# Setup of a fused attention and feed-forward kernel: the order of the small moves, of the value products and of GpSimd's work before the first block

## The reference, cut to what matters

```
x = x + L0_xattn(layernorm(x), ctx, mask)
q = hidden @ Wq.T + bq ; k = ctx @ Wk.T + bk ; v = ctx @ Wv.T + bv      # 16 heads of 16
attn = softmax(q k^T / sqrt(16) + mask) ; out = (attn @ v) @ Wo.T + bo
x = x + L0_ffn(layernorm(x))        # experts
x = x + L1_xattn(layernorm(x), ctx) # second attention
x = x + L1_ffn(layernorm(x))
```

## Time and profile before

| | us |
|---|---|
| median of three runs | 789.11 |
| lowest, highest | 788.72, 789.34 |
| the profiled execution, whole | 788.65 |
| its span in the trace | 786.4 |

### The profile page before, as it was taken

How to read it: one execution, slowest core, us unless ns; L and a number is a source line. 1 busy time by engine, 2 the same in 40 slices (tenths; PEclk the granted TensorE clock), 3 DMA queues, 4 the chain that set the end, 5 groups by cost and what they waited for, 6 DMA issues and landing times.

```text
span 786.4 us, 13553 instructions
## 1 busy us (share of the span) xinstructions
PE 730.7 (93%) x4372; PEld 548.4 (70%) x4372; DVE 645.4 (82%) x1546; ACT 513.6 (65%) x943; POOL 374.3 (48%) x323
## 2 busy tenths in 40 slices
PE   4799999999999999999998999999989999999995
PEld 3456666766558888888875555555558888888985
DVE  7658778777878878888887888998788999999995
ACT  3546556565654456555436777677778989989885
POOL 6374444334222223232214232222259999999884
PEclk9999999999999999999999999999999999999999
DMA  7975635564210000001047755755200000000001
GB/s 231 135 208 121 143 71 96 119 120 87 69 36 1 1 1 7 1 1 55 1 60 121 92 78 77 131 76 78 32 1 1 2 28 28 28 28 2 28 28 54
DMA packets 25101, 48.64 MB, mean 62 GB/s; under 512 B 3686, under 2 KB 7016, under 8 KB 24520
## 3 DMA queue, kind: packets, MB, share of 16 engines
q1 hardware_dynamic: 23366, 46.54, 30.6%
q10 hardware_dynamic: 1666, 1.24, 0.5%
HBM read 12.12 MB, written 4.19 MB: 21 GB/s over the span
## 4 chain that ended last, share of the span: by engine, by line
PE 53%; DVE 20%; issue 9%; ACT 7%; DMA 6%; POOL 4%; DVEq 0%; ACTq 0%; POOLq 0%
PE bank L141 15%; PE bank L649 7%; PE bank L413 6%; PE bank L436 6%; DMA qst<-mt 5%; PE bank L424 5%; PE bank L388 4%; DVE mx L342 4%; PE bank L416 3%; PE bank L812 3%; DVE fpart L768 3%; DVE x L617 2%; PE bank L391 2%; DVE fyl L780 2%; POOL fy L728 2%
## 5 line engine op out<-in xcount | busy, mean ns | idle before, releaser
L316 ACT ACTIVATE pt<-bank 77x512 f32<-77x512 f32 x256 | 141.0, 589 | 79.1 <-PE bank L416 59.3
L342 DVE TENSOR_REDUCE mx<-bank 128x4 f32<-128x308 f32 x256 | 108.6, 470 | 22.9 <-PE bank L391 12.3
L413 PE MATMUL bank<-qst,l_kst 128*77 128x512 f32 (+1 forms) x256 | 102.6, 416 | 16.8 <-DMA qst<-mt 10.5
L721 POOL TENSOR_TENSOR frise<-fg,fg 128x512 f32<-128x512 f32 x64 | 101.8, 1591 | 6.0 <-DVE fpart L768 0.8
L388 PE MATMUL bank<-l_kblk,qh 128*128 128x308 f32 x256 | 81.2, 339 | 7.6 <-DVE mx L342 6.4
L284 POOL TENSOR_TENSOR ol<-ot,oh 128x512 fp32r<-128x512 f32 x32 | 41.4, 1293 | 94.5 <-ACT oh L321 50.4
L103 POOL TENSOR_TENSOR rstd<-var,minus_half 128x4 f32<-128x4 f32 x32 | 34.8, 1088 | 102.5 <-DVE var L98 54.4
L617 DVE SCALAR_TENSOR_TENSOR x<-bank,eweight,x 128x256 f32<-128x256 f32 x192 | 79.5, 475 | 4.5 <-PE bank L649 4.2
L413 PEld LDWEIGHTS bank<-qst,l_kst 128*77 128x77 f32 (+1 forms) x256 | 36.5, 146 | 66.0 <-ACT pt L316 24.1
L114 ACT ACTIVATE xn<-x,shift,rstd 128x256 f32<-128x256 f32 (+1 forms) x128 | 67.0, 592 | 17.9 <-POOL shift L105 17.9
L812 PE MATMUL bank<-fw2h,fyh 128*128 128x256 f32 x256 | 73.3, 286 | 5.0 <-DVE fyl L780 4.7
(11 more groups left out here) (176 smaller groups left out, 2115.6 us busy)
## 6 DMA issues: line engine op xcount, KB each, us to landing
qst<-qh SPq DMA_DIRECT2D x64, 256.0 KB, 6.5
qst<-ql SPq DMA_DIRECT2D x32, 256.0 KB, 8.7
out<-x SPq DMA_DIRECT2D x8, 512.0 KB, 2.6
qst<-ml SPq DMA_DIRECT2D x8, 480.0 KB
x<-in_x SPq DMA_DIRECT2D x3, 1024.0 KB, 12.7
weights<-in_mlp_w SPq DMA_DIRECT2D x2, 1024.0 KB, 5.2
mraw<-in_mask SPq DMA_DIRECT2D x8, 154.0 KB
x<-in_x SPq DMA_DIRECT2D x2, 512.0 KB, 5.4
```

What stands on the lines that cost most here:

```text
L316: self.nc.scalar.activation(self.pt[0:T, i // 4 % 2, i % 4, :], self.bank_of(G, i)[0:T, :], ACT.Exp).then_inc(self.probs, 1)
L342: self.nc.vector.reduce_max(out, banks[u % len(banks)][:, 0:4 * T].rearrange("q (p par t) -> q p par t", p=2, par=2), AX.X).then_inc(self. ...
L413: last = self.nc.tensor.matmul(out, layer.kst[rows, layer.stack(c * HC + 2 * k + par), b * T:(b + 1) * T], self.qst[rows, self.slot(G), c ...
L721: self.nc.gpsimd.tensor_tensor(self.rise[:, k % 2, :], self.g1[:, k % self.R, :], self.g0[:, k % self.R, :], ALU.subtract).then_inc(self.r ...
```

## The change

Four engines' orders change; no instruction is added or dropped.

- SyncE: `load_mask` of block 1 and the move of block 0's maxima now come behind the first half (six `kst` copies and queries half 0); behind them the second half of the `kst` copies and queries half 1. The `x` loads stay behind those.
- GpSimd: the sixteen `kblk` instructions now wait for `kblk_ready` (the end of VectorE's own sixteen) in place of `kt_ready`, and come ahead of `invert(1)`; then `mask_parts(1)`, then `wol`. In the loop `mask_parts` is left out for G = 0.
- ScalarE: the first bank of values is copied ahead of `norm(1)`. In block 0 the two `leading` copies follow exponentials 1 and 2 in place of 0 and 1.
- TensorE: the value product of batch 0 comes ahead of block 0's queries, the other three stay. In block 0 the queries of block 1 follow scores 1 and 2 in place of 0 and 1.

```diff
@@ sync
                 for c in range(C):
+                    if c == 1:
+                        att.load_mask(sp, 1, d["mask"])
+                        att.stack_maxima(sp, 0)
                     for par in range(2):
                         ... # three kst copies
-                    if c == 0:
-                        att.stack_queries(sp, 0, 0)
-                att.stack_maxima(sp, 0)
-                att.stack_queries(sp, 0, 1)
-                att.load_mask(sp, 1, d["mask"])
+                    att.stack_queries(sp, 0, c)
@@ gpsimd
-                norm.invert(pool, 1)
-                pool.wait_ge(kt_ready, 1)
+                pool.wait_ge(kblk_ready, 1)
                 for head in range(H):
                     ... # kblk of batches 1 to 3
+                norm.invert(pool, 1)
+                att.mask_parts(pool, 1)
...
-                    if G + 1 < BLOCKS:
+                    if 0 < G < BLOCKS - 1:
                         att.mask_parts(pool, G + 1)
@@ scalar
-                norm.norm(act, 1)
-                act.wait_ge(v_clear, 2)
                 for k in range(2):
+                    if k == 1:
+                        norm.norm(act, 1)
+                    act.wait_ge(v_clear, 2)
                     act.wait_ge(v_done, k + 1)
...
-                        if h < C and n < BLOCKS:
+                        if G == 0 and h in (1, 2):
+                            att.leading(act, 1, h - 1)
+                        if G > 0 and h < C and n < BLOCKS:
                             att.leading(act, n, h)
@@ tensor
+                pe.wait_ge(vo_in, 64)
+                pe.wait_ge(cleared, 1)
+                values(0)
                 pe.wait_ge(wql_ready, 1)
...
                 att.turn_maxima(pe, 0, FIRST_MAX[0])
-                pe.wait_ge(vo_in, 64)
-                pe.wait_ge(cleared, 1)
-                for b in range(B):
-                    ... # one value product: four matmuls and a row of ones
+                for b in range(1, B):
+                    values(b)
...
-                        if i < C and n < BLOCKS:
+                        if G == 0 and i in (1, 2):
+                            att.queries(pe, l0, 1, i - 1)
+                        if G > 0 and i < C and n < BLOCKS:
                             att.queries(pe, l0, n, i)
```

More of the change, by code:

```diff
@@ L1504, in _, with values @@
                     norm.turn(pe, 0, c, att.W[c])
+                def values(b):
+                    bank = att.SC[b // 2][0:T, D * (b % 2):D * (b % 2) + D]
+                    for k in range(C):
+                        nc.tensor.matmul(bank, ctx[:, k, b * T:(b + 1) * T], wv0[:, k, :], start=(k == 0), stop=False)
+                    last = nc.tensor.matmul(bank, ones_row[:, :], rows[:], start=False, stop=True)
+                    if b % 2:
+                        last.then_inc(v_done, 1)
+                pe.wait_ge(vo_in, 64)
+                pe.wait_ge(cleared, 1)
+                values(0)
                 pe.wait_ge(wql_ready, 1)
```

## The result

The changed kernel takes 793.95 us in the median (792.96 to 795.41, 4 runs), the kernel before 788.91 beside it (787.91 to 789.34, 4 runs): ratio 1.0059 [1.0045, 1.0074], 5.0 us slower. The prediction was 787.4, in 783.0 to 790.2; the time lies above the range. It moved the way rival (c) said, and 2.7 us beyond that rival's 791.3.

The account below looks back on a forecast made before the run. It took score 0 of block 0, waiting for the maxima's move, and scarce DMA engines as the bound. Queue -2.6 and clock +0.9 gave -1.7 us: 788.65 to 786.95, median 0.46 above, so 787.4, range 783.0 to 790.2.

Parts of the forecast that it names:

- rival (c): Block 1's query copies become a burst at 127 instead of 191 GB/s: +2.2 us in sum, 791.3 us; chance 0.13.
- score 0 waited for the maxima's move behind the 47 rows: Block 0's head: with the maxima moved ahead, score 0 can start at 36.1 instead of 40.77, 4.7 us sooner.
- where each part of the setup would stand: Setup: `kblk` from 21.1 to 31.5, `norm(1)` from 32.9 to 35.0, transposes from 35.0 to 36.1 us.
- value product 0 holds up nothing: Ahead of block 0's queries: 1.6 us of work in TensorE's 2.08 us hole, costing nothing, at worst 0.3 us.
- the new bound of block 1's head is the DMA queue: Block 1's head: the maxima land behind its other copies in the same queue, so it starts at 62.0 us.
- a hole and a lower clock come back there: Ahead of block 1: a TensorE hole of 3.5 to 4.5 us, moved from block 0's head, with clock under 1 behind.
- queries half 1 later: Block 0: queries half 1 land by 42 us, score 8 needs them at 47, so 5 us of cover.
- the queue term, -2.6 us: Block 1's head: the DMA queue gets 2.6 us earlier, so block 1 starts at 62.0 instead of 64.59 us.
- the slow engine: Setup: a DMA engine some 2 us behind the others, expected to catch up its 2 us or more of lag.
- the clock, +0.9 us: Block 1's head: the moved hole brings the lower TensorE clock, costing 0.9 of the 1.4 us seen in block 0.

Follow-up runs that it names:

- e1: The kernel before with SyncE's part of the diff alone; ratio 1.0017 [1.0000, 1.0033].
- e2: The changed kernel with SyncE's old order; ratio 1.0008 [0.9998, 1.0017].
- e6: The kernel before with the 47 rows of `ml` moved in two DMAs of 45 and 2 rows in every block; ratio 1.0050 [1.0032, 1.0069].
- e3: The changed kernel with queries half 1 sent ahead of the second half of the `kst` copies; ratio 1.0067 [1.0054, 1.0080].
- e14: The changed kernel with `stack_low(1)`, the first of block 1's copies, held until all of `x` has landed; ratio 1.0046 [1.0032, 1.0060].
- e10: The changed kernel with `stack_low(1)`, the first of block 1's copies, held until VectorE's second `ql` of block 1; ratio 1.0036 [1.0019, 1.0053].
- e13: The changed kernel with the `x` loads behind block 1's maxima and `stack_low(1)` held until VectorE's second `ql` of block 1; ratio 0.9987 [0.9973, 1.0002].
- e7: The kernel before with the `x` loads alone moved behind block 1's maxima; ratio 1.0007 [0.9999, 1.0016].
- e4: The changed kernel with the two `x` loads (2 MB) moved behind block 1's maxima; ratio 0.9989 [0.9978, 1.0000].
- e9: The changed kernel with 12 unused matmuls of 512 columns ahead of block 1's score 0; ratio 1.0025 [1.0012, 1.0039].
- e8: The changed kernel with queries half 1 ahead of the second `kst` half and the `x` loads behind block 1's maxima; 789.50 us, ratio 1.0001 [0.9987, 1.0014].

## Why the prediction was wrong

**Right.** That score 0 waited for the maxima's move behind the 47 rows (e1, e2 and e6 show it from both sides); where each part of the setup would stand, to 0.5 us (the maxima were issued at 30.34 and not 29.9); that value product 0 holds up nothing (the first maximum unit starts at 21.21, before at 21.17); that the new bound of block 1's head is the DMA queue, since TensorE was through with block 0 and waited for the maxima; that a hole and a lower clock come back there.

**Failed: queries half 1 later, "That is 5 us of cover".** I asked who reads `qst` (score 8, at 47) and not who writes the buffer that the copy reads. `qh` has one buffer per half, and `leading` of block 1 needs it free. That user comes at 40.8. In after it costs 2.9 us of wait and the lower clock behind it, and takes the 4.6 us; e3, which sends queries half 1 first, has neither. The wait comes in every kernel that sends them late, the lower clock only in some. It moved the time of after little, since the queue was later still.

**Failed: the queue term, -2.6 us; it is +1.76.** This is the step that turned the sign. Two sizes in it were off. First, `x` was to be in at 46.5. The loads are issued at 36.86 and 37.47 and take up to 11.4 us:

```profile
DMA to landing us min/median/max: 9.1/10.2/11.4
```

That ends at 48.3 or later, and e14, whose SyncE waits for it, has 48.4: as good as before, 1.9 us over my figure. The prediction had the slow engine catch up in 30 to 40. No row shows that engine by itself; the share falls from 1.09 to 0.60, but the rate is 121 GB/s, where it was 128, so no more bytes were moved. Queries half 1 landed at 43.6, not by 41. Second, the rate. I took the 191 GB/s of the earlier trace rows for a property of the copies; 147 was measured. That is 1.62 MB in 50 to 61 in after, which at 191 would have taken 8.5 us instead of 11: +2.5 us, an estimate. 62.0 + 1.9 + 2.5 = 66.4, for 66.35. This is rival (c)'s mechanism, and the rate is just under the 150 GB/s that it named. What took the time past the +2.2 of (c) is that `x` came 1.9 us later than assumed, and the clock, at 2.7 instead of 1.4. The 1.28 MB by which (c) reckoned its price are in no row. A block's copies are 2.1 MB: four of `qh`, two of `ql`, one of 480 KB and the 47 rows with 94 KB. The page of before has their sizes (its counts are those of the whole program):

```profile
qst<-qh SPq DMA_DIRECT2D x64, 256.0 KB, 6.5
qst<-ql SPq DMA_DIRECT2D x32, 256.0 KB, 8.7
qst<-ml SPq DMA_DIRECT2D x8, 480.0 KB
```

I gave (c) 0.13 because "`stack_low` staggers the engines in every block of this layer". By e10, e13 and e14 the copies are fast where `stack_low` begins to move on engines that are idle, or all but one or two of them: 183 to 202 GB/s in six kernels (before, e1, e2, e7, e13, e14). They are slow where it comes behind traffic or is spread evenly, 131 to 152 in all others. So the mask sooner, which let the copies follow `x` "without a gap", took the faster copies away together with SyncE's order, and the 15 idle engines of 46 to 50, which I read as a waste, came with the fast ones.

**Failed: the clock, +0.9 us; it is +2.7.** I expected the hole of 4.25 us at block 0's head to reappear at block 1's with 0.9 of its 1.4 us. The price was read from one score with six query matmuls. In after the low clock lasts longer than that: 0.50 over 66 to 72, and a block that fills TensorE takes 24.01 instead of 21.30. Over all kernels, holes of 2.8 to 8.3 us were followed by 22.6 to 24.1, holes of up to 1.6 us by 21.3. Among the long ones the length doesn't tell the loss: 2.82 us in after cost 2.7, 3.92 us in e14 cost 1.6.

With the two terms as measured the sum is +1.76 + 2.71 = +4.5 us, for 5.0 in the medians.

**Open.** Why the same copies run at 183 to 202 GB/s from idle engines and at 131 to 152 otherwise. How far the engines are apart from each other would fit all the kernels, but no run shows it by itself. Why a hole or a wait of the same length is followed by the lower clock in one execution and not in another, or for longer. And why e4's gain of 1.9 us at block 2 is down to 0.25 us at 302 us in its profile; its clock is 0.83 in 225 to 235, where before has 1.00.

## What to carry to other kernels

When a copy is issued later, ask for two users: who reads what it writes, and who overwrites what it reads. A DMA rate read from a stretch belongs to what that stretch's queue looked like when the copies came; moving them into a full queue can cost more than the idle engines they were to fill. And where the critical engine is full, a hole ahead of it costs its length and then perhaps the slower clock behind it. So closing a hole that opens again further on can gain nothing or lose, and unused matmuls in it can pay.

## What the runs showed of the hardware

- The same copies within SBUF, 2.1 MB for a block, move at 183 to 202 GB/s or at 131 to 152 (54 to 60 us, or 43 to 56), with the DMA engines busy to 0.94 or more in either case, by what is under way when the first begins to move (152 in e10, 201 in e14). A busy share says nothing of which it is.
- Spreading 47 rows over more engines made the kernel 3.7 us slower (e6), though it took away the late engine and a third of SyncE's hold, and brought block 0's first score forward by 4.1 us.
- SyncE's issue of a pair of copies took 1.2 to 1.3 us in some places and 2.6 to 5.3 us in others, among them 3.88 us in e13, whose DMA engines had been empty until just before.
- A hole of TensorE of 2.82 us (after) was followed by a clock of 0.50 in 66 to 72 and 2.7 us lost in the block, one of 2.84 us (e9) by 0.72 and 1.3 us, one of 2.87 us (e8) by 1.5 us lost, one of 1.31 us (e4) by nothing.
